# A selective scan in quarters: its B and C rows spread by 32-row selections, the output products written over the states

## The chip, the core and the metric

One core of a Trainium2 chip runs the whole program. PE is TensorE (matmuls), PEld its weight loads, DVE is VectorE, ACT ScalarE, POOL GpSimd, SP SyncE, which here issues the DMAs. The metric is the device time of one execution in microseconds. All matmuls are in fp32, and each shows as two records in the trace, one behind the other.

## The reference

Twelve layers follow one another over x of 4 x 128 tokens and 128 features: four blocks of cross attention, a mixing layer and a feed-forward layer, each `x = x + layer(layernorm(x))`. The change concerns the mixing layer of block 0. With u, the output of a convolution, as 512 tokens of 128 features, it is:

```python
def _selective_scan(u, A_log, D_skip, W_dt, b_dt, W_B, W_C):
    A = -jnp.exp(A_log)
    dt = jax.nn.softplus(u @ W_dt + b_dt)
    Bt = u @ W_B
    Ct = u @ W_C

    def step(h, inp):
        dt_t, B_t, C_t, u_t = inp
        dA = jnp.exp(dt_t[..., None] * A)
        h = dA * h + (dt_t * u_t)[..., None] * B_t[:, None, :]
        y = jnp.einsum('bdn,bn->bd', h, C_t)
        return (h, y)
```

There are 16 states n for each feature, so B and C are 16 rows each over the tokens. The result is y plus u times D_skip, gated, and multiplied by w2.

## The kernel before

The features lie on the 128 partitions, the 4 x 128 tokens side by side in the columns. Everything is written out by hand: one program per engine, and semaphores between them. The stage between U and its result OT runs from about 134 to 198 us.

PE starts with dt's product (L1604). Then `spread(k)` (L1611) makes row n of B or C appear on all 128 partitions: a matmul whose weights are one column of W_B or W_C repeated 128 times, over the 512 columns of U. That takes a full 128-row matmul for each of the 32 rows. The results go round six PSUM banks, so a spread waits until DVE has taken the one six before it (`l0a_bc_taken`). `add_state` (L1617) sums the 16 products over the states, by identity matmuls into bank 1; each waits for its own product.

ACT turns dt (L912) into decays, one exponential over 512 columns per state (L541); POOL then zeroes the first column of each batch in them (L383), so that one scan can run over several states and batches.

DVE works in two halves of eight states. In each it multiplies eight spread B rows by dt times u into DBU (L922), scans all 4096 columns in one instruction, HS from DA and DBU (L926), and multiplies HS by the eight spread C rows, again into DBU (L930). As DBU serves twice, the second half's B products wait for the additions of the first (`l0a_added`). L934 and L937 finish the output once all 16 are added.

The order of PE's work is a list: 14 spreads, then an addition and a spread by turns. In each engine instructions run in the order written, and a wait holds up all that stands behind it. `PE.due(signal, lag=6)` means the count of signals so far less six.

Of the kernel before, what the change touches and what calls it, by code (L numbers as in the profile page):

```python
# [15 lines left out]
ALU = mybir.AluOpType  # L16
# [3 lines left out]
P = 128  # L20
# [69 lines left out]
def build(nc, d, cols, rows):  # L90

    with ExitStack() as ctx:
# [49 lines left out]
        def bank(k, rows_=P):  # L142
            return PSUM[0:rows_, k, :]
# [63 lines left out]
        HS = ARENA[:, 13568:13568 + 4096]  # L207
        SPREAD_BANKS = (4, 5, 6, 7, 0, 2)
# [154 lines left out]
        def _(gpsimd):  # L363
# [15 lines left out]
            for half in range(2):  # L379

                nc.gpsimd.wait_ge(sem("l0a_decay"), PO.due("l0a_decay"))
                cut = DA.rearrange("p (n t) -> p n t", t=P)[:, :, 0:1]
                nc.gpsimd.memset(cut, 0.0).then_inc(sem("l0a_decay_cut"), PO.sends("l0a_decay_cut"))  # L383
# [59 lines left out]
        def _(scalar):  # L443
# [93 lines left out]
            for half in range(2):  # L537
                if half:
                    nc.scalar.wait_ge(sem("l0a_scan"), AC.due("l0a_scan"))
                for n in range(8):  # L540
                    last = act(DA[:, n * 512:(n + 1) * 512], DT, ACT.Exp, scale=ANEG[:, half * 8 + n:half * 8 + n + 1])  # L541
                last.then_inc(sem("l0a_decay"), AC.sends("l0a_decay"))
# [196 lines left out]
        def _(vector):  # L739
# [169 lines left out]
            nc.vector.wait_ge(sem("l0a_preact"), DV.sent("l0a_preact"))  # L909
            nc.vector.wait_ge(sem("l0a_acts"), DV.due("l0a_acts"))  # L910
# [6 lines left out]
            for half in range(2):  # L917
                for n in range(8):
                    nc.vector.wait_ge(sem("l0a_bc"), DV.due("l0a_bc"))
                    if half:  # L920
                        nc.vector.wait_ge(sem("l0a_added"), DV.due("l0a_added"))
                    ve.tensor_tensor(DBU[:, n * 512:(n + 1) * 512], bank(SPREAD_BANKS[(n + half * 16) % 6]), DTU, ALU.mult)\  # L922
                        .then_inc(sem("l0a_bc_taken"), DV.sends("l0a_bc_taken"))
                nc.vector.wait_ge(sem("l0a_bc_taken"), DV.sent("l0a_bc_taken"))
                nc.vector.wait_ge(sem("l0a_decay_cut"), DV.due("l0a_decay_cut"))
                ve.tensor_tensor_scan(HS, DA, DBU, 0.0, ALU.mult, ALU.add).then_inc(sem("l0a_scan"), DV.sends("l0a_scan"))  # L926
                nc.vector.wait_ge(sem("l0a_scan"), DV.sent("l0a_scan"))
                for n in range(8):
                    nc.vector.wait_ge(sem("l0a_bc"), DV.due("l0a_bc"))
                    ve.tensor_tensor(DBU[:, n * 512:(n + 1) * 512], HS[:, n * 512:(n + 1) * 512],  # L930
                                     bank(SPREAD_BANKS[(n + 8 + half * 16) % 6]), ALU.mult)\
                        .then_inc(sem("l0a_bc_taken"), DV.sends("l0a_bc_taken"))
            nc.vector.wait_ge(sem("l0a_added"), DV.due("l0a_added", n=8))
# [494 lines left out]
        def _(tensor):  # L1428
# [175 lines left out]
            mm(bank(3), w("l0a_Wdt"), U, start=True, stop=True).then_inc(sem("l0a_product"), PE.sends("l0a_product"))  # L1604
            def spread(k):

                name, n = ("l0a_WB", "l0a_WC")[k // 8 % 2], k // 16 * 8 + k % 8
                due = PE.due("l0a_bc_taken", lag=6)
                if due is not None:
                    nc.tensor.wait_ge(sem("l0a_bc_taken"), due)  # L1610
                mm(bank(SPREAD_BANKS[k % 6]), w(name)[:, n:n + 1].broadcast_to([P, P]), U, start=True, stop=True)\  # L1611
                    .then_inc(sem("l0a_bc"), PE.sends("l0a_bc"))

            def add_state(half, n):

                nc.tensor.wait_ge(sem("l0a_bc_taken"), 16 * half + 8 + n + 1)
                mm(bank(1), ident, DBU[:, n * 512:(n + 1) * 512], start=half == 0 and n == 0,  # L1617
                    stop=half == 1 and n == 7, skip_group_check=True)\
                    .then_inc(sem("l0a_added"), PE.sends("l0a_added"))


            for half in range(2):
                for k in range(22 * half, 16 * half + 14):
                    spread(k)
                for n in range(8):
                    add_state(half, n)
                    if 16 * half + 14 + n < 32:
                        spread(16 * half + 14 + n)
# [460 lines left out]
def lay_out(i):  # L2089
# [12 lines left out]
    def spread(bias):  # L2102
        out = np.zeros((4, 32, 4), np.float32)
        out[:, :HD, :] = bias.reshape(4, 4, HD).transpose(1, 2, 0)
        return out.reshape(P, 4)
# [12 lines left out]
         ("l0a_Wdt", i["L0_attn_W_dt"]), ("l0a_WB", i["L0_attn_W_B"]), ("l0a_WC", i["L0_attn_W_C"]),  # L2118
# [96 lines left out]
```

## Time and profile before

| what | value |
|---|---|
| runs | 1321.06, 1321.3, 1321.06 us, median 1321.06 |
| profiled execution | 1319.12 us |
| its span | 1317.3 us |
| mean granted clock of TensorE | 0.889 |
| PE busy | 1123.8 us, 85% of the span |
| DVE busy | 619.5 us, 47% |
| ACT busy | 425.8 us, 32% |
| the two scans (L926) | 17.4 us together |
| spreads (L1611), 32 matmuls | 32.7 us |
| additions (L1617), 16 matmuls | 18.5 us |

The span runs from the first to the last instruction in the profile; the execution's time also holds what lies around it. A record's mean length is not the distance to the next one, since neighbouring records overlap on every engine. The granted clock is a share of 2.4 GHz; it has two levels here, 1.00 and 0.50 (1.2 GHz), and a mean in between says how much of a stretch each had.

### The profile page before, as it was taken

How to read it: one execution, taken by the hardware profiler on the slowest of the kernel's cores; microseconds unless marked ns; L12 is line 12 of the kernel's file. 1: busy time of each engine (PE TensorE's matmuls, PEld its weight loads, DVE VectorE, ACT ScalarE, POOL GpSimd, SP SyncE). 2: the span in 40 equal slices, each digit the busy share in tenths (PEclk: the TensorE clock that was granted, in tenths of full speed). 3: DMA queues.
4: the chain of work that ended last, by engine and by line, in shares of the span. 5: the costliest groups of instructions: out<-in, count | busy, mean ns of one | idle time of the engine just before them, and what ended most of it. 6: DMA issues, size and time to landing. Idle time of an engine off the chain costs nothing.

```text
span 1317.3 us, 13027 instructions
## 1 busy us (share of the span) xinstructions
PE 1123.8 (85%) x4766; PEld 642.5 (49%) x4766; DVE 619.5 (47%) x1075; ACT 425.8 (32%) x586; POOL 314.4 (24%) x95
## 2 busy tenths in 40 slices
PE   7996789956899966775867999999999999998558
PEld 4663335734666624443746444544454445444434
DVE  4885754143598842223533443343434344342345
ACT  3663404314465551321125322222322331232011
POOL 0000000000000000000000666556655663665000
PEclk9997789966799985886889999899989998998569
DMA  8100000030000020032000000000000000000100
GB/s 345 76 0 1 0 0 0 1 127 1 0 1 0 1 97 0 0 136 104 1 0 0 17 20 20 15 15 21 20 12 16 20 20 8 21 20 0 70 1 8
DMA packets 21366, 40.15 MB, mean 30 GB/s; under 512 B 2496, under 2 KB 18880, under 8 KB 19648
## 3 DMA queue, kind: packets, MB, share of 16 engines
q1 hardware_dynamic: 21312, 39.41, 8.1%
q8 instruction: 36, 0.59, 0.2%
q14 instruction: 18, 0.15, 0.0%
HBM read 39.14 MB, written 0.26 MB: 30 GB/s over the span
## 4 chain that ended last, share of the span: by engine, by line
PE 78%; DVE 12%; ACT 7%; issue 2%; POOL 1%; DMA 0%; POOLq 0%; DVEq 0%; ACTq 0%
PE PSUM L1933 16%; PE PSUM L1937 16%; PE PSUM L1451 9%; PE PSUM L1659 2%; PE PSUM L1670 2%; PE PSUM L1483 2%; PE PSUM L1962 2%; PE PSUM L1968 1%; PE PSUM L1460 1%; DVE ARENA L926 1%; PE PSUM L2043 1%; PE PSUM L1617 1%; DVE HN L754 1%; PE PSUM L1503 1%; PE PSUM L1518 1%
## 5 line engine op out<-in xcount | busy, mean ns | idle before, releaser
L424 POOL TENSOR_TENSOR ARENA<-ARENA 128x2048 f32<-128x2048 f32 x64 | 288.7, 4511 | 196.6 <-ACT ARENA L684 196.6
L1292 DVE TENSOR_TENSOR ARENA<-PSUM,RK 128x512 f32<-128x512 f32 x256 | 175.7, 691 | 271.8 <-PE PSUM L1933 270.1
L1933 PE MATMUL PSUM<-ARENA,CK 128*128 128x512 f32 x512 | 257.3, 606 | 5.1 <-DVE ARENA L1292 4.3
L1937 PE MATMUL PSUM<-ARENA,CK 128*128 128x512 f32 x512 | 253.0, 597 | 5.8 <-ACT ARENA L706 3.7
L684 ACT ACTIVATE ARENA<-ARENA,CK 128x2048 f32<-128x2048 f32 x64 | 128.1, 2002 | 350.0 <-DVE ARENA L1292 350.0
L1937 PEld LDWEIGHTS PSUM<-ARENA,CK 128*128 128x128 f32 x512 | 97.4, 191 | 132.1 <-issue 112.2
L1933 PEld LDWEIGHTS PSUM<-ARENA,CK 128*128 128x128 f32 x512 | 97.7, 194 | 126.2 <-issue 98.1
L366 POOL TENSOR_TENSOR RSTD<-VE,MHALF 128x4 f32<-128x4 f32 x17 | 17.1, 1009 | 554.5 <-DVE VE L751 554.5
L1451 PE MATMUL PSUM<-WK,CT 128*128 128x512 f32 x256 | 124.1, 607 | 0.0
L454 ACT ACTIVATE SQ<-PSUM 128x512 f32<-128x512 f32 x128 | 76.2, 597 | 67.2 <-PE PSUM L1451 59.4
L773 DVE TENSOR_REDUCE RK<-SQ 128x8 f32<-128x512 f32 x128 | 84.8, 682 | 14.1 <-ACT SQ L454 12.0
L1433 PE MATMUL PSUM<-WA,HN 128*128 128x128 f32 x52 | 14.0, 422 | 79.6 <-DVE HN L754 79.6
L1451 PEld LDWEIGHTS PSUM<-WK,CT 128*128 128x128 f32 x256 | 43.6, 190 | 33.3 <-issue 24.6
L1433 PEld LDWEIGHTS PSUM<-WA,HN 128*128 128x128 f32 x52 | 9.0, 211 | 83.1 <-DVE HN L754 57.9
L446 ACT ACTIVATE HT<-PSUM 128x512 f32<-128x512 f32 x10 | 6.0, 596 | 95.3 <-PE PSUM L1433 95.2
L1611 PE MATMUL PSUM<-ARENA,WB 128*128 128x512 f32 x64 | 32.7, 648 | 0.0
L563 ACT ACTIVATE ARENA<-PSUM,WB 128x512 f32<-128x512 f32 x32 | 22.0, 687 | 29.1 <-PE PSUM L1659 28.3
L1670 PEld LDWEIGHTS PSUM<-CK,ARENA 128*128 128x128 f32 x256 | 29.7, 192 | 3.4 <-issue 3.4
L1659 PE MATMUL PSUM<-HT,CK 128*128 128x512 f32 x64 | 30.9, 610 | 0.0
L1670 PE MATMUL PSUM<-CK,ARENA 128*128 128x128 f32 x256 | 29.7, 275 | 0.0
L987 DVE SCALAR_TENSOR_TENSOR ACC<-PSUM,SM,ACC 128x128 f32<-128x128 f32 x32 | 9.0, 344 | 43.4 <-PE PSUM L1670 43.4
L1617 PE MATMUL PSUM<-ARENA,WA 128*128 128x512 f32 x32 | 18.5, 690 | 11.8 <-DVE ARENA L930 11.8
(388 smaller groups left out, 1412.5 us busy)
## 6 DMA issues: line engine op xcount, KB each, us to landing
CT<-in_ctxT SPq DMA_DIRECT2D x4, 1024.0 KB, 10.9
CK<-in_l0f_experts SPq DMA_DIRECT2D x1, 4096.0 KB, 23.6
CK<-in_ctxk SPq DMA_DIRECT2D x1, 4096.0 KB, 12.1
ARENA<-in_l2f_experts SPq DMA_DIRECT2D x2, 2048.0 KB, 8.2
CK<-in_ctxT SPq DMA_DIRECT2D x64, 64.0 KB, 1.8
CK<-in_ctxr SPq DMA_DIRECT2D x64, 64.0 KB, 1.8
ARENA<-in_l2f_experts SPq DMA_DIRECT2D x1, 3072.0 KB, 14.2
WB<-in_wb SPq DMA_DIRECT2D x1, 2802.5 KB, 11.9
```

Source lines behind the costliest of these rows:

```text
L424: nc.gpsimd.tensor_tensor(LS[b % 2], LS[b % 2], PR[:, k % 2, :], ALU.add)\
L454: act(SQ[:, m % 2, :], bank(5 + 2 * (m % 2)), ACT.Square).then_inc(sem("key_squares"), AC.sends("key_squares"))
L684: act(PR[:, k % 2, :], PR[:, k % 2, :], ACT.Exp, bias=SHIFT).then_inc(sem("l3x_probs"), AC.sends("l3x_probs"))
L773: ve.tensor_reduce(RK[:, m * 8:(m + 1) * 8], SQ[:, m % 2, :].rearrange("p (h e) -> p h e", e=DH), AX.X, ALU.add).then_inc(sem("key_norm"), ...
L1292: ve.tensor_tensor(PR[:, k % 2, c * 512:(c + 1) * 512].rearrange("p (j n) -> p j n", j=4), PSUM[:, c % 2, :].rearrange("p (j n) -> p j n", ...
L1451: mm(bank(5 + 2 * c), CT[:, t * P:(t + 1) * P], WK[:, c * 512:(c + 1) * 512], start=True, stop=True).then_inc(sem("key_rows"), PE.sends("k ...
L1611: mm(bank(SPREAD_BANKS[k % 6]), w(name)[:, n:n + 1].broadcast_to([P, P]), U, start=True, stop=True)\
L1617: mm(bank(1), ident, DBU[:, n * 512:(n + 1) * 512], start=half == 0 and n == 0, stop=half == 1 and n == 7, skip_group_check=True)\
L1659: mm(bank(1 + c % 2), E2[:, e * NW + c * P:e * NW + (c + 1) * P], HT[:, :], start=True, stop=True)\
L1670: last = mm(PSUM[:, 3 + e % 2, b * P:(b + 1) * P], HB[:, e % 2, c, b * P:(b + 1) * P], E2[:, at:at + P], start=c == 0, stop=c == FC - 1)
L1933: mm(bank(c % 2), CTT[:, k, :], qpb[:, b, c * 512:(c + 1) * 512], start=True, stop=True)\
L1937: return mm(bank(4 + c), CKT[:, k, :], PR[:, k % 2, c * 512:(c + 1) * 512], start=first, stop=final, skip_group_check=True)
```

## The change

- The 16 columns each of W_B and W_C lie side by side in one weight, WBC of 32 columns. Four matmuls make B and C of U once for each group of 32 partitions (L1614 of the changed kernel), all into bank 4; DVE copies them to BC (L914).
- A spread is now a matmul over 32 rows of BC, with one column of the identity's 32 x 32 block, repeated 128 times, as weights (L1624). Spread k uses the partitions of row group k mod 4, and four in a row use four groups.
- The scan runs in quarters of four states (2048 columns). DA, DBU and HS have two places each for them. ACT's decays for a quarter wait for the scan two quarters back; POOL's memset comes four times.
- The C products are written over HS (L939), and the additions read HS. DBU waits for no addition any more; the scan of the third and fourth quarter waits for the additions of the quarter two back.
- PE's list is new, as shown below.

```diff
+        BC = ARENA[:, 4736:4736 + 512]
...
-            for half in range(2):
+            for q in range(4):
 
                 nc.gpsimd.wait_ge(sem("l0a_decay"), PO.due("l0a_decay"))
-                cut = DA.rearrange("p (n t) -> p n t", t=P)[:, :, 0:1]
+                cut = DA[:, q % 2 * 2048:(q % 2 + 1) * 2048].rearrange("p (n t) -> p n t", t=P)[:, :, 0:1]
...
-            for half in range(2):
-                if half:
-                    nc.scalar.wait_ge(sem("l0a_scan"), AC.due("l0a_scan"))
-                for n in range(8):
-                    last = act(DA[:, n * 512:(n + 1) * 512], DT, ACT.Exp, scale=ANEG[:, half * 8 + n:half * 8 + n + 1])
+            for q in range(4):
+                due = AC.due("l0a_scan", lag=2)
+                if due is not None:
+                    nc.scalar.wait_ge(sem("l0a_scan"), due)
+                for n in range(4):
+                    at = (q % 2 * 4 + n) * 512
+                    last = act(DA[:, at:at + 512], DT, ACT.Exp, scale=ANEG[:, q * 4 + n:q * 4 + n + 1])
                 last.then_inc(sem("l0a_decay"), AC.sends("l0a_decay"))
...
+            nc.vector.wait_ge(sem("l0a_product"), DV.due("l0a_product"))
+            ve.tensor_copy(BC, bank(4)).then_inc(sem("l0a_bc_rows"), DV.sends("l0a_bc_rows"))
             nc.vector.wait_ge(sem("l0a_acts"), DV.due("l0a_acts"))
...
-            for half in range(2):
-                for n in range(8):
+            for q in range(4):
+                half = slice(q % 2 * 2048, (q % 2 + 1) * 2048)
+                for n in range(4):
+                    at = (q % 2 * 4 + n) * 512
                     nc.vector.wait_ge(sem("l0a_bc"), DV.due("l0a_bc"))
-                    if half:
-                        nc.vector.wait_ge(sem("l0a_added"), DV.due("l0a_added"))
-                    ve.tensor_tensor(DBU[:, n * 512:(n + 1) * 512], bank(SPREAD_BANKS[(n + half * 16) % 6]), DTU, ALU.mult)\
+                    ve.tensor_tensor(DBU[:, at:at + 512], bank(SPREAD_BANKS[(q * 8 + n) % 6]), DTU, ALU.mult)\
                         .then_inc(sem("l0a_bc_taken"), DV.sends("l0a_bc_taken"))
                 nc.vector.wait_ge(sem("l0a_bc_taken"), DV.sent("l0a_bc_taken"))
                 nc.vector.wait_ge(sem("l0a_decay_cut"), DV.due("l0a_decay_cut"))
-                ve.tensor_tensor_scan(HS, DA, DBU, 0.0, ALU.mult, ALU.add).then_inc(sem("l0a_scan"), DV.sends("l0a_scan"))
+                if q >= 2:
+                    nc.vector.wait_ge(sem("l0a_added"), 4 * (q - 1))
+                ve.tensor_tensor_scan(HS[:, half], DA[:, half], DBU[:, half], 0.0, ALU.mult, ALU.add)\
+                    .then_inc(sem("l0a_scan"), DV.sends("l0a_scan"))
                 nc.vector.wait_ge(sem("l0a_scan"), DV.sent("l0a_scan"))
-                for n in range(8):
+                for n in range(4):
+                    at = (q % 2 * 4 + n) * 512
                     nc.vector.wait_ge(sem("l0a_bc"), DV.due("l0a_bc"))
-                    ve.tensor_tensor(DBU[:, n * 512:(n + 1) * 512], HS[:, n * 512:(n + 1) * 512],
-                                     bank(SPREAD_BANKS[(n + 8 + half * 16) % 6]), ALU.mult)\
+                    ve.tensor_tensor(HS[:, at:at + 512], HS[:, at:at + 512], bank(SPREAD_BANKS[(q * 8 + 4 + n) % 6]), ALU.mult)\
                         .then_inc(sem("l0a_bc_taken"), DV.sends("l0a_bc_taken"))
...
+            for j in range(4):
+                last = mm(PSUM[32 * j:32 * j + 32, 4, :], w("l0a_WBC"), U, start=True, stop=True)
+            last.then_inc(sem("l0a_product"), PE.sends("l0a_product"))
+
             def spread(k):
 
-                name, n = ("l0a_WB", "l0a_WC")[k // 8 % 2], k // 16 * 8 + k % 8
+                n = k // 4 % 2 * N + k // 8 * 4 + k % 4
                 due = PE.due("l0a_bc_taken", lag=6)
                 if due is not None:
                     nc.tensor.wait_ge(sem("l0a_bc_taken"), due)
-                mm(bank(SPREAD_BANKS[k % 6]), w(name)[:, n:n + 1].broadcast_to([P, P]), U, start=True, stop=True)\
-                    .then_inc(sem("l0a_bc"), PE.sends("l0a_bc"))
...
+                r = 32 * (k % 4)
+                mm(bank(SPREAD_BANKS[k % 6]), ident[r:r + 32, r + n:r + n + 1].broadcast_to([32, P]), BC[r:r + 32, :],
+                   start=True, stop=True).then_inc(sem("l0a_bc"), PE.sends("l0a_bc"))
+
+            def add_state(q, n):
+
+                nc.tensor.wait_ge(sem("l0a_bc_taken"), 8 * q + 4 + n + 1)
+                at = (q % 2 * 4 + n) * 512
+                mm(bank(1), ident, HS[:, at:at + 512], start=q == 0 and n == 0, stop=q == 3 and n == 3, skip_group_check=True)\
                     .then_inc(sem("l0a_added"), PE.sends("l0a_added"))
 
-
-            for half in range(2):
-                for k in range(22 * half, 16 * half + 14):
-                    spread(k)
-                for n in range(8):
-                    add_state(half, n)
-                    if 16 * half + 14 + n < 32:
-                        spread(16 * half + 14 + n)
+            nc.tensor.wait_ge(sem("l0a_bc_rows"), PE.due("l0a_bc_rows"))
+            for k in range(8):
+                spread(k)
+            for q in range(4):
+                for n in range(4):
+                    if q < 3:
+                        spread(8 * (q + 1) + n)
+                    add_state(q, n)
+                for n in range(4):
+                    if q < 3:
+                        spread(8 * (q + 1) + 4 + n)
```

PE's list in this stage before: the product for dt, spreads (L1611) and additions (L1617), up to w2's product (L1439).

```order
L1604 MATMUL PSUM<-ARENA,WB 128x512
L1611 MATMUL PSUM<-ARENA,WB 128x512 x14
L1617 MATMUL PSUM<-ARENA,WA 128x512
L1611 MATMUL PSUM<-ARENA,WB 128x512
...
L1617 MATMUL PSUM<-ARENA,WA 128x512
L1611 MATMUL PSUM<-ARENA,WB 128x512 x9
L1617 MATMUL PSUM<-ARENA,WA 128x512
L1611 MATMUL PSUM<-ARENA,WB 128x512
...
L1617 MATMUL PSUM<-ARENA,WA 128x512 x6
L1439 MATMUL PSUM<-WB,OT 128x128 x4
```

The same place in the changed kernel: WBC is L1614, a spread L1624, an addition L1631.

```order
L1612 MATMUL PSUM<-ARENA,WB 128x512
L1614 MATMUL PSUM<-ARENA,WB 32x512 x4
L1624 MATMUL PSUM<-ARENA,WA 128x512 x9
L1631 MATMUL PSUM<-ARENA,WA 128x512
L1624 MATMUL PSUM<-ARENA,WA 128x512
...
L1631 MATMUL PSUM<-ARENA,WA 128x512
L1624 MATMUL PSUM<-ARENA,WA 128x512 x5
L1631 MATMUL PSUM<-ARENA,WA 128x512
...
L1624 MATMUL PSUM<-ARENA,WA 128x512 x4
L1631 MATMUL PSUM<-ARENA,WA 128x512 x4
L1447 MATMUL PSUM<-WB,OT 128x128 x4
```

Nine spreads stand ahead of the first addition. Then come three pairs of an addition and a spread, a fourth addition, and five spreads in a row (three times, the last time four), and four additions at the end.

DVE's list before: B products (L922), scan (L926), C products (L930).

```order
L922 TENSOR_TENSOR ARENA<-PSUM,ARENA 128x512 x8
L926 SCALAR_TENSOR_TENSOR ARENA<-ARENA 128x4096
L930 TENSOR_TENSOR ARENA<-ARENA,PSUM 128x512 x8
...
L934 SCALAR_TENSOR_TENSOR ARENA<-ARENA,WB,PSUM 128x512
L937 SCALAR_TENSOR_TENSOR OT<-ARENA 128x512
```

And in the changed kernel, from the copy to BC (L914) on.

```order
L914 COPY ARENA<-PSUM 128x512
L917 SCALAR_TENSOR_TENSOR ARENA<-ARENA 128x512
L920 TENSOR_TENSOR ARENA<-ARENA 128x512
L927 TENSOR_TENSOR ARENA<-PSUM,ARENA 128x512 x4
L933 SCALAR_TENSOR_TENSOR ARENA<-ARENA 128x2048
L939 TENSOR_TENSOR ARENA<-ARENA,PSUM 128x512 x4
...
L942 SCALAR_TENSOR_TENSOR ARENA<-ARENA,WB,PSUM 128x512
L945 SCALAR_TENSOR_TENSOR OT<-ARENA 128x512
```

The triple of products, scan and products stands four times now, with half as much in each part, and the copy is one operation more.

## Rows read from the trace of the kernel before

**Rows 1.** The page: the span, and the chain that ended last, by engine.
```profile
span 1317.3 us, 13027 instructions
...
PE 78%; DVE 12%; ACT 7%; issue 2%; POOL 1%; DMA 0%; POOLq 0%; DVEq 0%; ACTq 0%
```

**Rows 2.** Chain of waits, 120 to 210 us: start us, length us, what, how many.
```profile
142.51 5.02 ACT ARENA L541 x8
147.84 8.70 DVE ARENA L926
...
157.30 2.07 PE PSUM L1617 x2
...
160.67 0.86 PE PSUM L1617 x2
...
171.83 2.59 PE PSUM L1611 x6
174.44 0.70 DVE ARENA L922
175.17 8.70 DVE ARENA L926
...
184.63 2.08 PE PSUM L1617 x2
186.71 1.71 PE PSUM L1611 x2
...
196.59 0.76 DVE ARENA L934
```

**Rows 3.** Table by stage: length, busy us of each engine, granted clock (PEclk), DMA share, GB/s.
```profile
156.53:160.12 3.59, 2.82 (x4) 1.26 (x5) 3.56 (x6) 3.56 (x6) 0.00 (x0) 0.50 0.00 0
183.87:190.84 6.97, 6.21 (x8) 2.59 (x9) 4.36 (x7) 0.00 (x0) 0.00 (x0) 0.51 0.00 0
190.84:196.59 5.75, 5.71 (x14) 2.25 (x12) 0.69 (x1) 0.00 (x0) 0.00 (x0) 1.00 0.00 0
```

**Rows 4.** Groups by form: line, what, count | busy us, mean ns | idle before, releaser.
```profile
L926 DVE TENSOR_TENSOR_SCAN ARENA<-ARENA 128x4096 f32<-128x4096 f32 x2 | 17.4, 8692 | 0.2 <-POOL ARENA L383 0.2
...
L541 ACT ACTIVATE ARENA<-ARENA,SM 128x512 f32<-128x512 f32 x16 | 10.0, 708 | 9.1 <-DVE ARENA L926 9.0
...
L912 DVE SCALAR_TENSOR_TENSOR ARENA<-ARENA 128x512 f32<-128x512 f32 x1 | 0.7, 693 | 3.4 <-ACT ARENA L535 3.4
...
L1159 DVE TENSOR_TENSOR_SCAN ARENA<-ARENA 16x512 f32<-16x512 f32 x1 | 1.2, 1211 | 0.0
```

**Rows 5.** Timeline of the stage, DVE: start us, length us, what, count.
```profile
142.75 4.87 DVE L922 TENSOR_TENSOR ARENA<-PSUM,ARENA 128x512 f32<-128x512 f32 x8
```

**Rows 6.** Timeline, 481.6 to 486.2 us, PE: 32-row and 128-row matmuls by turns.
```profile
482.73 1.13 PE L1771 MATMUL PSUM<-HT,WB 128*128 128x512 f32 x2
...
483.78 1.70 PE L1764 MATMUL PSUM<-ARENA,WB 32*128 32x512 f32 x4
```

**Rows 7.** Timeline, 200 to 320 us, PE: four row groups, then 128 rows.
```profile
297.71 2.09 PE L1483 MATMUL PSUM<-ARENA,QT 8*128 8x512 f32 x8
299.73 3.77 PE L1503 MATMUL PSUM<-WA,ARENA 128*128 128x128 f32 x16
```

**Rows 8.** PE after two idle times: timeline around 495 and 599 us, then table by stage.
```profile
494.90 0.64 PE L1774 MATMUL PSUM<-SM,WA 128*128 128x32 f32 x2 [2.78 <-ACT ARENA L599]
...
599.12 1.12 PE L1812 MATMUL PSUM<-ARENA,WB 128*128 128x512 f32 x2 [3.53 <-DVE ARENA L1159]
...
494.70:495.60 0.90, 0.64 (x2) 0.50 (x2) 0.03 (x1) 0.72 (x3) 0.00 (x0) 0.50 0.00 0
599.10:600.40 1.30, 1.28 (x3) 0.52 (x4) 0.00 (x0) 0.00 (x0) 0.00 (x0) 1.00 0.75 287
600.50:602.00 1.50, 1.50 (x2) 0.00 (x0) 0.00 (x0) 0.00 (x0) 0.00 (x0) 0.50 0.91 265
```

More of the change, by code:

```diff
@@ L925, in _ @@
                 nc.vector.wait_ge(sem("l0a_decay_cut"), DV.due("l0a_decay_cut"))
-                ve.tensor_tensor_scan(HS, DA, DBU, 0.0, ALU.mult, ALU.add).then_inc(sem("l0a_scan"), DV.sends("l0a_scan"))
+                if q >= 2:
+                    nc.vector.wait_ge(sem("l0a_added"), 4 * (q - 1))
+                ve.tensor_tensor_scan(HS[:, half], DA[:, half], DBU[:, half], 0.0, ALU.mult, ALU.add)\
+                    .then_inc(sem("l0a_scan"), DV.sends("l0a_scan"))
                 nc.vector.wait_ge(sem("l0a_scan"), DV.sent("l0a_scan"))
-                for n in range(8):
+                for n in range(4):
+                    at = (q % 2 * 4 + n) * 512
                     nc.vector.wait_ge(sem("l0a_bc"), DV.due("l0a_bc"))
-                    ve.tensor_tensor(DBU[:, n * 512:(n + 1) * 512], HS[:, n * 512:(n + 1) * 512],
-                                     bank(SPREAD_BANKS[(n + 8 + half * 16) % 6]), ALU.mult)\
+                    ve.tensor_tensor(HS[:, at:at + 512], HS[:, at:at + 512], bank(SPREAD_BANKS[(q * 8 + 4 + n) % 6]), ALU.mult)\
                         .then_inc(sem("l0a_bc_taken"), DV.sends("l0a_bc_taken"))
-            nc.vector.wait_ge(sem("l0a_added"), DV.due("l0a_added", n=8))
+            nc.vector.wait_ge(sem("l0a_added"), DV.due("l0a_added", n=16))
             ve.scalar_tensor_tensor(out=Y0, in0=U, scalar=w("l0a_D"), in1=bank(1), op0=ALU.mult, op1=ALU.add)\
@@ L1610, in spread @@
                     nc.tensor.wait_ge(sem("l0a_bc_taken"), due)
-                mm(bank(SPREAD_BANKS[k % 6]), w(name)[:, n:n + 1].broadcast_to([P, P]), U, start=True, stop=True)\
-                    .then_inc(sem("l0a_bc"), PE.sends("l0a_bc"))
[L1614 to L1618, printed above, removed]
-                    .then_inc(sem("l0a_added"), PE.sends("l0a_added"))
-            for half in range(2):
-                for k in range(22 * half, 16 * half + 14):
-                    spread(k)
-                for n in range(8):
-                    add_state(half, n)
-                    if 16 * half + 14 + n < 32:
-                        spread(16 * half + 14 + n)
+                r = 32 * (k % 4)
[5 more added lines that the diff above has]
+                mm(bank(1), ident, HS[:, at:at + 512], start=q == 0 and n == 0, stop=q == 3 and n == 3, skip_group_check=True)\
+                    .then_inc(sem("l0a_added"), PE.sends("l0a_added"))
+            nc.tensor.wait_ge(sem("l0a_bc_rows"), PE.due("l0a_bc_rows"))
[9 more added lines that the diff above has]
+                        spread(8 * (q + 1) + 4 + n)
             nc.tensor.wait_ge(sem("l0a_y"), PE.due("l0a_y"))
@@ L2117, in lay_out @@
          ("l0a_w1", i["L0_attn_w1_w"]), ("l0a_v1", i["L0_attn_v1_w"]), ("l0a_w2", i["L0_attn_w2_w"]),
-         ("l0a_Wdt", i["L0_attn_W_dt"]), ("l0a_WB", i["L0_attn_W_B"]), ("l0a_WC", i["L0_attn_W_C"]),
+         ("l0a_Wdt", i["L0_attn_W_dt"]), ("l0a_WBC", np.concatenate([i["L0_attn_W_B"], i["L0_attn_W_C"]], axis=1)),
          ("l0a_Alog", i["L0_attn_A_log"]), ("l0a_conv", i["L0_attn_conv_w"].reshape(P, 3)),
```

## The prediction

> **What bounds the kernel now.** First the page: PE makes up 78% of the chain that ended last, DVE 12% [rows 1]. That is an average over twelve layers. The change touches one of them, the selective scan, so everything below is read from 134 to 200 us. In the chain of waits for that stretch [rows 2] the reader sees DVE and PE take turns: eight decays on ACT, a scan on DVE (8.70 us), then PE's additions and spreads one behind another until 174.44, the second scan, and PE again until DVE's L934 at 196.59. So neither engine bounds the stage alone. While DVE scans PE runs dry, and after the scan DVE waits for PE. The table by stage [rows 3] gives the third fact: PE ran out of work in both scans and came back at a granted clock of 0.50 (1.2 GHz) both times, for 2.8 us (157.30 to 160.12) and for 6.2 us (184.63 to 190.84), and then had 1.00 (2.4 GHz) again.
>
> The stage falls into four stretches, and I price the change by them: up to the first scan (147.84), two scans of 8.69, one gap between them (156.53 to 175.17, 18.64 us) and the tail from the second scan's end to L934 (183.87 to 196.59, 12.72 us).
>
> **Before the first scan.** New in front are four 32-column products of U (WBC), a copy of them to BC on DVE, and the first spreads, which now wait for that copy. WBC can follow L1604's stream at about 136.7. Its nearest row is four groups at once on half clock, 2.09 us [rows 7], so it is done by 138.8; the copy costs 0.69 like the other DVE operations of this size and ends at 139.5, in DVE's idle time before L912 (3.4 us, waiting for ACT) [rows 4]. Spreads 0 to 3, one in each row group, take another 2.09 and are there at 141.7. DVE asks for the first at 142.75. So these edits are covered with 1 us to spare; if the four did not run side by side, they would take four times 1.71 and the fourth product would be some 2 us late. The scan now needs four decays instead of eight: 142.51 + 3 x 0.61 + 0.71 = 145.05, and from the last decay to the scan passes 0.32, through POOL's memset, as before (147.52 to 147.84) [rows 2, 4]. The four products are ready at 145.2. First scan at 145.4: **-2.5 us**. The second quarter's decays run on under the scan, the third's and fourth's (2.6 us each) wait only for a scan two back and fit under the next one; POOL has four short memsets for two.
>
> **The scans.** Two lengths stand in the trace: 4096 columns 8.692 us and 512 columns (on 16 partitions) 1.211 us [rows 4]. That is 2.087 ns a column and 0.14 fixed, so 4.42 for 2048. Four make 17.67 for 17.38: **+0.3 us**. DVE's 32 products stay 32, at 0.60 each when nothing is late (eight in 4.87) [rows 5]. Writing in place over the states gives them no other size; it lets quarter q+2's scan wait for quarter q's four additions, long done.
>
> **The gaps: three where there was one.** The order on PE decides here. An addition cannot start before its C product, and a spread of the next quarter stands behind each addition: spread 8, add, 9, add, 10, add, 11. Spread 8 runs early, under the scan. The next scan needs the product on spread 11, so each gap holds DVE's first C product and its handoffs (0.03 + 0.68 + 0.05 = 0.75), then six PE steps in a row (add, 9, add, 10, add, 11), then handoff, product, handoff (0.04 + 0.69 + 0.04 = 0.77). Only spreads 12 to 15 stand together, and they run under a scan, where PE had time anyway. So the four row groups shorten nothing in the gap.
> A step between unlike shapes costs more than one between like ones. Like shapes follow at 0.86 on full clock and 1.71 on half [rows 2]. Between 32-row and 128-row matmuls the starts stand 1.05 apart on full clock (482.73 to 483.78) [rows 6] and 2.02 on half (297.71 to 299.73, rows of 8 to 128) [rows 7]. The last step ends 1.13 after its start on full clock, 2.07 on half. A gap is 0.75 + 5 x 1.05 + 1.13 + 0.77 = 7.9 at full clock and 0.75 + 5 x 2.02 + 2.07 + 0.77 = 13.7 at half. Three gaps less the old one: +5.1 or +22.5.
> The Trainium skill, TensorEngine Tiling (Array Packing), section Available Configurations, says that a change of the tiling mode (not of the tile) drains TensorE; the trace agrees in that a switch costs 0.19 more than a like step, though less than a full drain would. A full drain, estimated by that rule with a record's length of 1.13 per step in place of 1.05, would make a gap 8.3 and the sum below 1.2 us larger.
>
> **The tail.** The last quarter has four additions where 22 matmuls' worth of mixed work stood: 0.75 + 4 x 0.86 + 0.3 = 4.5 on full clock, 8.0 on half, for 12.72: -8.2 or -4.7.
>
> **Which clock.** At full clock throughout: -2.5 + 0.3 + 5.1 - 8.2 = **-5.3**. At half clock throughout: -2.5 + 0.3 + 22.5 - 4.7 = **+15.6**. Those are the ends. In each quarter PE has spreads 12 to 15 and 16 after the scan has begun, some 2 us, and then nothing for 4.42 - 2.0 + 0.75 = 3.2 us. The rows nearest to this length are an idle of 2.78 us (PE came back at 0.50) and one of 3.53 us (it came back at 1.00 and had 0.50 some 1.3 us later) [rows 8]. So I take it that the clock falls once in each scan, for about as long as after the two scans of before: the mean of 2.8 and 6.2, 4.5 us. In 4.5 us of half clock 2.2 steps are done that would take 2.3 us at full clock, so 2.2 us are lost, four times: -5.3 + 8.8 = **+3.5**. With 2.8 us each time it is +0.1, with 6.2 us +6.7.
>
> **The sum.** The profiled execution took 1319.12 us, its span of 1317.3 and 1.8 around it, and stands 1.9 under the median of the three runs, 1321.06. With +3.5 it would be 1322.6, and the median 1324.5. What follows the stage is the same code, later by that much; the clock changes there too (it is 0.50 in several stretches after idling [rows 8]), and where its falls land can move by a few microseconds either way. That is in the range.
>
> **Rivals.**
> A, the clock holds: the scans are short enough now that PE keeps 2.4 GHz. For it: idle falls from 5.1 and 6.7 us to 3.2, and after 3.53 us PE did come back at 1.00 [rows 8]. Against: it fell right after, and 2.78 us was enough elsewhere. -5.3, so 1315.8. This is the case on the other side; it decides below some 2.8 us of half clock per gap, where the sum changes sign.
> B, the clock does not come back within a gap: it took 6.2 us of unbroken work after 184.63 [rows 3], and a gap's work is broken at each switch. +15.6, so 1336.7.
> C, switches cost nothing with 32 full rows: steps of 0.86 and 1.71. A gap loses 5 x 0.19 + 0.1 = 1.05 at full clock and some 1.6 at half, about 3.8 in three: 3.5 - 3.8, so 1320.8. Against it stand the rows of L1764 and L1771, which are this very shape.
> D, the change does what its form suggests: PE is always ahead and DVE runs through. Gap 8 x 0.60 + 0.15 = 4.95, three 14.9: -2.5 + 0.3 - 3.7 - 8.2 = -14.1, so 1307. Against it is the order on PE, which lets no spread pass an addition.
>
> **How the numbers follow.** Forecast 0.56, A 0.15, B 0.13, C 0.08, D 0.04, later stages shifting by more than this one 0.04. The predicted time is the forecast's, 1324.5. The range 1315 to 1332 takes in A, C and the forecast with 2.8 to 6.2 us (1321.2 to 1327.8) and a few microseconds of the later stages, and leaves out B and D. Runs differ by 0.02% here, but I call same what lies within 0.2% (2.6 us), about what a measurement can tell. Faster: A 0.15, D 0.04, 0.02 of C, 0.03 of the forecast and the rest: 0.24. Same: the forecast with short falls of the clock 0.20 and most of C: 0.26. Slower: the rest of the forecast 0.35, B 0.13, 0.02 of the rest: 0.50.
>
> **What would show it.** Right: the first scan at 145.4 (covering wrong: later than 146); scans of 4.4; the distance from a scan's end to the next scan 9 to 12 us; PE's starts in the gap 1.05 or 2.02 apart, add and spread by turns; DVE's waits before its B products (L927), not before its C products; the clock at 0.50 at each first addition. Gaps of 8 with the clock at 1.00 mean A, gaps near 14 mean B, starts 0.86 apart mean C, gaps of 5 mean D. The forecast is wrong if PE takes the spreads out of turn, or if L934 comes before 193 or after 206.

## The result and the profile after

The changed kernel takes 1331.79 us (median of 4 runs, 1330.11 to 1333.04), the kernel before 1321.18 beside it (4 runs): ratio 1.0081, 95% interval [1.0066, 1.0096]. It is slower by 10.6 us, where +3.5 was forecast. The profiled execution took 1331.16 us, its span is 1329.4. First the page: the span and the chain that ended last, by engine.

```profile
span 1329.4 us, 13044 instructions
...
PE 78%; DVE 12%; ACT 7%; issue 2%; POOL 1%; DMA 0%; POOLq 0%; DVEq 0%; ACTq 0%
```

These shares are those of [rows 1], and say nothing of the 12.1 us between the spans. The chain of waits of the stage shows where the time went (start us, length us, what, how many).

```profile
137.57 1.56 PE PSUM L1612 x2
...
147.41 4.43 DVE ARENA L933
151.87 0.70 DVE ARENA L939
152.61 2.08 PE PSUM L1631 x2
154.69 2.00 PE PSUM L1624 x2
156.69 2.01 PE PSUM L1631 x2
...
162.70 2.02 PE PSUM L1624 x2
164.74 0.70 DVE ARENA L927
165.47 4.43 DVE ARENA L933
...
182.05 4.43 DVE ARENA L933
...
198.21 4.43 DVE ARENA L933
202.66 0.70 DVE ARENA L939
203.40 5.19 PE PSUM L1631 x8
208.62 0.76 DVE ARENA L942
```

L1612 is the product for dt (L1604 before), L933 a scan, L939 a C product, L1631 an addition, L1624 a spread, L927 a B product, L942 what L934 was. The reader sees six PE steps in a row between a C product and the next scan's last B product, three times, where [rows 2] have one gap. From the dt product on I cut the stage as the prediction did (us):

| | before | after | difference |
|---|---|---|---|
| dt product to first scan | 12.83 | 9.84 | -3.0 |
| scans | 17.39 | 17.72 | +0.3 |
| gaps | 18.64 | 13.63 + 12.16 + 11.73 = 37.52 | +18.9 |
| last scan's end to L934 or L942 | 12.73 | 5.99 | -6.7 |
| stage | 61.59 | 71.04 | +9.45 |
| from there to the end | 1120.73 | 1120.75 | 0.0 |

The other 2.6 us lie ahead of the stage, in unchanged code (the dt product starts at 137.57, before at 135.00). In the profiles of the twelve runs below, whose code is the same up to there, it starts anywhere from 134.96 to 138.29, so nothing ties those 2.6 us to the change.

The clock that each gap had is in the table by stage of the changed kernel (stretch, length, busy us of PE, PEld, DVE, ACT and POOL, granted clock, DMA share, GB/s).

```profile
151.84:165.47 13.63, 12.86 (x13) 3.50 (x14) 5.16 (x9) 2.56 (x4) 0.12 (x1) 0.50 0.00 0
...
168.90:172.30 3.40, 2.44 (x6) 0.59 (x4) 3.37 (x5) 2.38 (x4) 0.00 (x0) 1.00 0.00 0
172.30:182.05 9.75, 9.75 (x11) 2.50 (x10) 2.78 (x5) 0.18 (x1) 0.12 (x1) 0.50 0.01 2
185.90:189.30 3.40, 2.68 (x6) 0.59 (x4) 3.37 (x6) 0.00 (x0) 0.00 (x0) 1.00 0.00 0
189.30:198.21 8.91, 8.91 (x10) 2.50 (x10) 2.28 (x5) 0.00 (x0) 0.00 (x0) 0.50 0.00 0
```

The first gap passes at 0.50 from end to end. The second has 1.00 for one step and part of the next, the third for two steps; then both have 0.50 again, for 9.75 and 8.91 us, although PE is busy in all of that time. Compare [rows 3], where the clock was back after 6.2 us of work behind the second scan. The timeline of PE shows the same (start us, length us, line, operation, count, idle before).

```profile
167.65 2.05 PE L1624 MATMUL PSUM<-ARENA,WA 32*128 32x512 f32 x6
170.67 1.13 PE L1631 MATMUL PSUM<-ARENA,WA 128*128 128x512 f32 x2 [0.96 <-DVE ARENA L939]
171.72 1.55 PE L1624 MATMUL PSUM<-ARENA,WA 32*128 32x512 f32 x2
173.21 2.08 PE L1631 MATMUL PSUM<-ARENA,WA 128*128 128x512 f32 x2
175.21 2.07 PE L1624 MATMUL PSUM<-ARENA,WA 32*128 32x512 f32 x2
```

Starts are 1.05 apart (170.67 to 171.72), then 1.49 where the clock falls, then 2.00 (173.21 to 175.21). Before the first additions of the three gaps and the tail PE idled 4.82, 0.96, 0.72 and 1.93 us, in this order. The rest of the sum stands in the groups by form (count | busy us, mean ns | idle before, releaser).

```profile
L933 DVE TENSOR_TENSOR_SCAN ARENA<-ARENA 128x2048 f32<-128x2048 f32 x4 | 17.7, 4424 | 0.3 <-POOL ARENA L384 0.2
L927 DVE TENSOR_TENSOR ARENA<-PSUM,ARENA 128x512 f32<-128x512 f32 x16 | 10.7, 686 | 22.0 <-PE PSUM L1624 21.9
...
L917 DVE SCALAR_TENSOR_TENSOR ARENA<-ARENA 128x512 f32<-128x512 f32 x1 | 0.7, 692 | 1.5 <-ACT ARENA L536 1.5
L914 DVE COPY ARENA<-PSUM 128x512 f32<-128x512 f32 x1 | 0.7, 691 | 1.1 <-PE PSUM L1614 1.1
```

DVE waits 21.9 us for spreads (L1624) ahead of its B products, and nowhere else in the loop but for 0.2 us ahead of the first scan. The copy (L914) took 0.69 and behind it DVE still idled 1.5 us for ACT, so the copy lies in idle time.

### The profile page after: what moved, and what is told of

Same layout as the page of the kernel before. It is cut to its first block, busy times and chain, and to the rows that moved or that the text cites. A ratio compares the mean times of both kernels' runs of the same rounds, so it can differ in the third digit from the quotient of the medians.

```text
span 1329.4 us, 13044 instructions
## 1 busy us (share of the span) xinstructions
PE 1135.1 (85%) x4774; PEld 638.6 (48%) x4774; DVE 620.4 (47%) x1078; ACT 425.8 (32%) x586; POOL 314.6 (24%) x97
## 4 chain that ended last, share of the span: by engine, by line
PE 78%; DVE 12%; ACT 7%; issue 2%; POOL 1%; DMA 0%; POOLq 0%; DVEq 0%; ACTq 0%
PE PSUM L1949 16%; PE PSUM L1953 16%; PE PSUM L1459 9%; PE PSUM L1675 2%; PE PSUM L1686 2%; PE PSUM L1491 2%; PE PSUM L1631 2%; PE PSUM L1978 1%; PE PSUM L1468 1%; DVE ARENA L933 1%; PE PSUM L1984 1%; PE PSUM L2059 1%; DVE HN L757 1%; PE PSUM L1624 1%; PE PSUM L1511 1%
## 5 line engine op out<-in xcount | busy, mean ns | idle before, releaser
L1631 PE MATMUL PSUM<-ARENA,WA 128*128 128x512 f32 x32 | 28.2, 996 | 8.4 <-DVE ARENA L939 8.4
L1624 PE MATMUL PSUM<-ARENA,WA 32*128 32x512 f32 x64 | 29.9, 944 | 2.5 <-DVE ARENA L927 1.6
## 6 DMA issues: line engine op xcount, KB each, us to landing
ARENA<-in_l2f_experts SPq DMA_DIRECT2D x1, 3072.0 KB, 14.1
```

Source lines behind the costliest of these rows:

```text
L1624: mm(bank(SPREAD_BANKS[k % 6]), ident[r:r + 32, r + n:r + n + 1].broadcast_to([32, P]), BC[r:r + 32, :], start=True, stop=True).then_inc(s ...
L1631: mm(bank(1), ident, HS[:, at:at + 512], start=q == 0 and n == 0, stop=q == 3 and n == 3, skip_group_check=True)\
```

## The experiments

Two things can be at fault: the six serial steps that the order on PE puts into each gap (theory S), and the clock at which PE runs them. "Full spreads" are the 128-row ones of the kernel before, "lead" is the time from the dt product to the first scan, "tail" that from the last scan's end to L942 (L934 before). All kernels are changes of the kernel after or of the kernel before, as said.

**e1_block: the four spreads ahead of the four additions.**

```diff
                 for n in range(4):
                     if q < 3:
                         spread(8 * (q + 1) + n)
+                for n in range(4):
                     add_state(q, n)
```

> The change with PE's list altered alone: the next quarter's four B spreads stand ahead of the four additions instead of between them. If the six serial steps of a gap are the cause (theory S), spreads 10 and 11 follow the first C products at once and a gap falls from about 12 to 13.6 us to DVE's own 8 x 0.60 + 0.15 = 5.0; the stage from L1612 to L942, 71.1 us in the change and 61.6 before, becomes 47 to 51, and the kernel is 10 to 14 us faster than before. If 32-row matmuls and their switches cost by themselves (theory R), or the shorter scans do (theory Q), it stays within 4 us of the change.

Measured: 1307.99 against 1320.09, ratio 0.9897 [0.9877, 0.9918]. Gaps 4.95, 5.53, 4.95, stage 48.56. The stage is 22.5 us shorter than in the kernel after, for a change of order alone. Chain of waits of e1_block around the first gap:

```profile
147.81 4.44 DVE ARENA L933
...
153.01 2.67 PE PSUM L1624 x4
155.68 5.39 PE PSUM L1631 x8
161.08 1.15 PE PSUM L1624 x8
162.23 2.48 DVE ARENA L939 x4
...
167.14 4.44 DVE ARENA L933
```

And from DVE's timeline of e1_block the two places where it waited for C spreads (in brackets the idle time before, and for what):

```profile
162.23 2.48 DVE L939 TENSOR_TENSOR ARENA<-ARENA,PSUM 128x512 f32<-128x512 f32 x4 [0.62 <-PE PSUM L1624]
...
182.13 2.48 DVE L939 TENSOR_TENSOR ARENA<-ARENA,PSUM 128x512 f32<-128x512 f32 x4 [1.20 <-PE PSUM L1624]
```

Between 153 and 162 the chain is on PE, yet the second scan (157.18 to 161.61) passes beside it and is not on the chain. DVE is held only for 0.62 us after that scan, and for 1.20 us after the fourth, where C spreads stand behind additions. Theory S holds, and rival D of the prediction is what this order gives: a gap of 4.95, as D had it.

**e2_full_rows: the order of the change, every spread a 128-row matmul.**

```diff
-                r = 32 * (k % 4)
-                mm(bank(SPREAD_BANKS[k % 6]), ident[r:r + 32, r + n:r + n + 1].broadcast_to([32, P]), BC[r:r + 32, :],
+                mm(bank(SPREAD_BANKS[k % 6]), w("l0a_WBC")[:, n:n + 1].broadcast_to([P, P]), U,
```

> The change with its order, but each spread a 128-row matmul over U as before (the BC product and copy stay and are not used), so PE changes shape nowhere in the gap. Theory R: the gaps shrink by most of what was lost, to below 6 us. Theory S: a gap keeps its six steps, of 0.86 at full clock or 1.71 at half: 6.9 or 12.1 us; as five spreads in a row now fill 4.3 us of each scan, I expect full clock, some 7 us a gap after the first, and a first scan some 2 us later. Stage 54 to 58 us, kernel 3 to 8 us faster than before.

Measured: 1309.02, 0.9905 [0.9883, 0.9927]. Gaps 6.96, 6.95, 6.96, tail 4.51, stage 54.05. Chain of waits of e2_full_rows, first gap:

```profile
151.13 1.12 PE PSUM L1630 x2
152.25 0.86 PE PSUM L1623 x2
...
155.69 0.87 PE PSUM L1623 x2
156.58 0.70 DVE ARENA L927
```

The six steps are there still, at 0.86 each, and the clock has 1.00 from 143.3 to the end of the stage. So in this order the 32-row spreads cost 17.0 us of stage: 3.0 by the switches (7.93, the gap at full clock in e3 below, for 6.95, three times), 13.7 in the gaps and 1.5 in the tail by the clock, less 1.1 that they gain before the first scan. Timeline of PE in e2_full_rows, first addition of the second gap:

```profile
162.51 1.12 PE L1630 MATMUL PSUM<-ARENA,WA 128*128 128x512 f32 x2 [0.81 <-DVE ARENA L939]
```

PE idles 1.68, 0.81, 0.81 and 1.67 us before the three gaps and the tail here, and keeps 1.00; the changed kernel idled 0.96 and 0.72 before its last two gaps and lost it. So the length of the idle time does not tell the two apart. What differs is what PE ran: 128-row matmuls alone, or 32-row ones among them.

**e3_fill: work that keeps the clock, order and shapes of the change.** Five 128-row matmuls ahead of the first addition of quarter 0 and three ahead of that of each later quarter write to a bank that nothing reads (extra work).

```diff
                         spread(8 * (q + 1) + n)
+                    if n == 0:
+                        for _ in range(5 if q == 0 else 3):
+                            mm(bank(3), ident, U, start=True, stop=True)
                     add_state(q, n)
```

> The change with fill: five 128-row matmuls of 512 columns into an unused bank ahead of the first addition, three ahead of the first addition of each later quarter. They are extra work in PE's idle time under the scans. If the half clock after each idle time is what made the forecast too small (theory S with the clock), the granted clock stays 1.00 in the gaps, steps are 1.05 and gaps 7.9, and the stage is some 55 to 58 us, 13 us less than in the change. If the clock has no part in it, the stage gets no shorter, or longer by what the fill sticks out from the scans (up to 5 us).

Measured: 1316.49, 0.9968 [0.9957, 0.9980]. Gaps 10.69, 7.93, 7.93, tail 4.51, the clock 1.00 from 153.7 on. The stage is 59.11, a little over the 55 to 58 expected, since the first gap still had extra work in it that began at 0.50. With 7.93 there too the stage would be 59.11 - 2.76 = 56.35, 5.2 less than before: that is the prediction's -5.3 for a held clock, and its 7.9 a gap. Work for nothing makes the kernel 15 us faster than the change.

**e4_halves_rows: the 32-row spreads alone, in the kernel before.** WBC, its copy and the selection spreads are put in; halves, order and DBU stay.

```diff
-                name, n = ("l0a_WB", "l0a_WC")[k // 8 % 2], k // 16 * 8 + k % 8
+                n = k // 8 % 2 * N + k // 16 * 8 + k % 8
...
-                mm(bank(SPREAD_BANKS[k % 6]), w(name)[:, n:n + 1].broadcast_to([P, P]), U, start=True, stop=True)\
+                r = 32 * (k % 4)
+                mm(bank(SPREAD_BANKS[k % 6]), ident[r:r + 32, r + n:r + n + 1].broadcast_to([32, P]), BC[r:r + 32, :],
+                   start=True, stop=True).then_inc(sem("l0a_bc"), PE.sends("l0a_bc"))
```

> The kernel before with one part of the change: B and C in 32 rows on four row groups, spread by selections; halves, PE's order and the place of the products as before. Theory R and theory S with its switch price: sixteen steps that change shape each time in the gap and six in the tail cost 0.19 more on full clock and 0.31 on half, so 3 to 6 us more, and more where the clock is at half for longer; kernel slower than before by 3 to 9 us. If the four row groups speed up PE on the path, it is faster than before.

Measured: 1339.32, 1.0133 [1.0109, 1.0158]: 19 us slower, where 3 to 9 were expected. The stage is 80.85, and the one gap is 34.85 where it was 18.64. Table by stage of e4_halves_rows: the spreads before the first addition, the gap, and the nine spreads that end it.

```profile
142.46:152.33 9.87, 9.87 (x28) 5.16 (x28) 8.11 (x11) 7.67 (x11) 0.15 (x1) 0.50 0.00 0
159.18:194.03 34.85, 34.08 (x45) 9.68 (x46) 10.40 (x17) 5.01 (x8) 0.15 (x1) 0.50 0.00 0
190.00:196.12 6.12, 6.12 (x19) 2.68 (x18) 3.98 (x4) 0.00 (x0) 0.00 (x0) 0.50 0.00 0
```

PE is busy for 34.08 of 34.85 us and stays at 0.50. Additions and spreads by turns make up 30.1 us of it (159.95 to 190.00, fifteen steps of 2.00). In the kernel before, the same order of like shapes had 1.00 again after 2.8 us [rows 3]. But the first and last lines show 32-row spreads with no addition between them, 9.9 and 6.1 us long, and the clock stays at 0.50 there too. It was 1.00 again only at about 214.6 us, 3.1 us after the last additions began to stand together.

**e5_halves_64 and e6_rows_fill: is it the few rows, and do turns of the two shapes lose a clock that they have?** e5 is e4 with spreads of 64 rows in two groups. e6 is e4 with 128-row matmuls for nothing ahead of the first addition, six in the first half, five in the second (extra work).

```diff
 e5
-                r = 32 * (k % 4)
-                mm(bank(SPREAD_BANKS[k % 6]), ident[r:r + 32, r + n:r + n + 1].broadcast_to([32, P]), BC[r:r + 32, :],
+                r = 64 * (k % 2)
+                mm(bank(SPREAD_BANKS[k % 6]), ident[r:r + 64, r + n:r + n + 1].broadcast_to([64, P]), BC[r:r + 64, :],
 e6
+                for _ in range(6 - half):
+                    mm(bank(3), ident, U, start=True, stop=True)
                 for n in range(8):
                     add_state(half, n)
```

> As e4_halves_rows, in which the clock stayed at 0.50 from before the stage to its end, but each spread over 64 rows (two row groups) instead of 32; the numbers computed are the same. If the pause at each switch of shape keeps the clock down, it stays at 0.50 as in e4: steps 2.0, gap 35 us. If the narrow matmuls do, 64 rows are nearer to 128 and the clock may come back in the gap: some steps of 1.05 and a gap well under 30 us.

> As e4_halves_rows, with six and five 128-row matmuls of 512 columns as extra work ahead of the first addition of each half, under the scans. If the half clock alone makes e4's gap 34.9 us, and alternation at full clock does not lose it, the steps are 1.05 and the gap is 0.75 + 16 x 1.05 + some 2 us = 18.5 to 20, with a stage of 62 to 66 us. If alternation itself makes the clock fall, it shows 0.50 again within the gap and the gap stays above 25 us.

Measured, one run each: e5 1340.12, gap 35.26; e6 1322.1, gap 19.64. Table by stage of e5_halves_64:

```profile
153.90:191.50 37.60, 33.51 (x38) 9.02 (x40) 13.11 (x16) 5.01 (x8) 0.15 (x1) 0.50 0.00 0
191.50:198.30 6.80, 2.78 (x12) 0.95 (x8) 6.52 (x2) 0.00 (x0) 0.00 (x0) 1.00 0.00 0
```

And of e6_rows_fill, its gap, and most of its tail:

```profile
158.88:178.51 19.63, 19.52 (x48) 5.70 (x46) 10.30 (x16) 5.01 (x8) 0.15 (x1) 1.00 0.00 1
187.10:200.70 13.60, 12.72 (x14) 4.12 (x15) 5.16 (x9) 0.00 (x0) 0.00 (x0) 0.50 0.00 0
```

With twice the rows the clock stays down just as long while the shapes alternate (157.99 to 188.04, again 30.1 us). In e5 it came back at 191.5, 3.5 us after the last addition had ended, in a run of 64-row spreads; in e4 it did not come back in such a run of 32-row ones. So e5 doesn't clear the few rows: 64 may be too few as well. Against few rows alone as the cause stands the changed kernel, where the clock came back within 2.3 and 2.7 us of five 32-row spreads in a row (from 166.64 and from 183.23). Which of the two holds the clock down, few rows or the turns, stays open.

In e6 the turns began at 1.00, right behind 128-row work, and held it for 19.6 us, with starts 1.05 apart. That isn't a rule either: in the changed kernel they began at 1.00 twice, behind 0.96 and 0.72 us of idle time, and lost it within two steps. In e6's own second half five matmuls were too few: PE idled 3.84 us behind them, the additions started at 0.50, and the tail took 16.58. The share of pauses doesn't tell the two clocks apart: at 0.50 an unlike step costs 2.00 us against 1.71 for a like one, some 15% of PE's time; at 1.00 it is 1.05 against 0.86, which is no less.

**e7_before_fill: the kernel before, clock held.** The two lines of e6 in the kernel before (extra work).

> The kernel before with that fill alone (six and five matmuls under the two scans). Before lost 2.8 and 6.2 us at half clock after its scans, which is 1.4 and 3.1 us of work. With the clock held the gap falls from 18.6 to about 17.3 us and the tail from 12.7 to 9.6, so the kernel is 4 to 5 us faster than before. If the clock is not what the stage loses there, nothing changes.

Measured: 1314.43 against 1320.4, 0.9951 [0.9934, 0.9968]; gap 17.26 and tail 9.67 for 18.64 and 12.73. Table by stage, gap and tail:

```profile
158.40:176.00 17.60, 16.78 (x39) 7.52 (x40) 10.84 (x18) 5.01 (x8) 0.15 (x1) 1.00 0.00 1
184.00:194.00 10.00, 9.21 (x21) 3.72 (x20) 5.35 (x9) 0.00 (x0) 0.00 (x0) 1.00 0.00 0
```

The stage is 57.15, and the medians are 6.0 apart. So the clock cost the kernel before 4.4 us in this stage, 1.4 behind the first scan and 3.1 behind the second, as expected.

**e8_adds_last: all eight spreads of the next quarter, then the additions.**

```diff
-                for n in range(4):
+                for n in range(8):
                     if q < 3:
                         spread(8 * (q + 1) + n)
+                for n in range(4):
                     add_state(q, n)
-                for n in range(4):
-                    if q < 3:
-                        spread(8 * (q + 1) + 4 + n)
```

> The change with PE's list as: all eight spreads of the next quarter, then the four additions of this one, which then run under the next scan. As e1_block, but no C product should wait for a spread behind additions (e1 waited 0.6 and 1.2 us there). Gaps 4.95 each, tail 4.5 at full clock to 8 at half, stage 47 to 50 us, for 48.6 in e1; kernel 11 to 14 us faster than before.

Measured: 1304.09, 0.9891 [0.9866, 0.9916]; gaps 4.95, 6.01, 4.93, tail 5.97, stage 49.28. The second gap is 1.1 longer than the 4.95 expected of each: no C product waits for a spread any more, but a B product of the third quarter does, 0.98 us, behind the first four additions, which ran mostly at 0.50.

**e9_last_full: the same order, full spreads.** The edit of e2 in e8.

> The order of e8 (all eight spreads of the next quarter, then the four additions), with every spread a 128-row matmul over U as in e2. WBC and its copy are still made and nothing reads the copy. Theory (once the order is right, four row groups pay, because PE's work per quarter has to fit DVE's): DVE needs 4.42 + 4.95 = 9.4 us a quarter, PE 12 like steps of 0.86 = 10.3 at full clock, so PE becomes the bound by about 1 us a quarter, gaps 5.5 to 6.5, but PE never idles and keeps 1.00; lead 11.0 as in e2, tail 4.5. Stage 11.0 + 17.7 + 18 + 4.5 = 51, total 1304 to 1308. Rival (the four row groups are worth nothing in any order): gaps 4.95 and the tail 4.5, stage 48, total under 1304, at least as fast as e8.

Measured: 1307.45 against 1320.75, 0.9916 [0.9888, 0.9944]; gaps 4.95, 4.95, 5.38, tail 5.15, stage 49.16. Chain of waits of e9_last_full:

```profile
151.37 5.42 PE PSUM L1623 x12
156.78 3.43 PE PSUM L1630 x8
160.22 6.87 PE PSUM L1623 x16
167.08 3.43 PE PSUM L1630 x8
170.52 6.87 PE PSUM L1623 x16
177.38 6.88 PE PSUM L1630 x16
...
184.29 0.76 DVE ARENA L942
```

PE is the bound without a break for 32.9 us, 10.3 a quarter, as the theory said, but it had worked ahead by enough that this shows only in the third gap (+0.4) and in the tail (5.15 for 4.5). The stage is as long as e8's. There the row groups gain 1.3 us in the lead (9.71 for 11.04), and half clock takes it back in the second gap and the tail: e8 has 0.50 until about 161.3 and again from 175.6 to 181.8. So neither theory got its number: 49.2 stands between 51 and 48. In this order the row groups are worth nothing in the stage, and in the order of the change they cost 17.0 us. Whether the 3 to 4 us between the totals of e9 and e8 are theirs stays open, since they lie behind the stage (last entry).

**e10_in_place: the output products in place, alone, in the kernel before.**

```diff
-                    if half:
-                        nc.vector.wait_ge(sem("l0a_added"), DV.due("l0a_added"))
...
+                if half:
+                    nc.vector.wait_ge(sem("l0a_added"), DV.due("l0a_added", n=8))
                 ve.tensor_tensor_scan(HS, DA, DBU, 0.0, ALU.mult, ALU.add).then_inc(sem("l0a_scan"), DV.sends("l0a_scan"))
...
-                    ve.tensor_tensor(DBU[:, n * 512:(n + 1) * 512], HS[:, n * 512:(n + 1) * 512],
+                    ve.tensor_tensor(HS[:, n * 512:(n + 1) * 512], HS[:, n * 512:(n + 1) * 512],
...
-                mm(bank(1), ident, DBU[:, n * 512:(n + 1) * 512], start=half == 0 and n == 0,
+                mm(bank(1), ident, HS[:, n * 512:(n + 1) * 512], start=half == 0 and n == 0,
```

> The kernel before with only the output products written in place over the states (HS): the additions read HS, the second half's B products wait for no addition, its scan waits for the eight additions. Theory (PE's order sets the gap, and the wait that moves was never the last one): gap 18.6, tail 12.7, stage 61.6, total within 0.2% of before. Rival (the wait of the B products on the additions held DVE, or the scan's new wait holds it longer): a gap at least 1 us shorter or longer.

Measured: 1320.72 against 1320.75, 1.0017 [0.9994, 1.0039], 10 runs; stage 60.56 (gap 19.08, tail 11.25; the clock comes back later in the gap and earlier in the tail than in the kernel before). Within the 0.4% of the interval, writing in place costs and gives nothing here.

**e11_last_again and e12_block_again: e8 and e1 on one chip.**

> The kernel of e8 once more, in more rounds and on the same chip as e12. Theory: stage 49.3, total 1302 to 1307, and within 2 us of e12, since the two stages differ by less than 1 us. Rival (additions last are worth more than they save in the stage): 3 to 4 us faster than e12, as the two medians stood apart.

> The kernel of e1 once more, beside e11. Theory: stage 48.6, total 1304 to 1308. Rival: as under e11, 1308 with e11 at 1304.

Measured: e11 1303.67, 0.9888 [0.9865, 0.9912], stage 49.98; e12 1306.29, 0.9901 [0.9878, 0.9925], stage 49.07; 6 runs each. The medians stand 2.6 apart, between the two expectations, and the intervals overlap: the best version is one of the two, 14 to 17 us faster than before and, by the medians, 25 to 28 faster than the change. The same code gave stages 0.5 (e1, e12) and 0.7 us (e8, e11) apart, so less than that between two stages says nothing.

The runs of e12 lie in two heaps (1303.43, 1303.99, 1304.77 and 1307.80, 1307.91, 1308.10). The profiled runs of e1 and e12, the same kernel, fell one in each heap, and tell where they part: L942 is followed by 1119.46 us in e1 and 1114.84 in e12. Counted from the start of each span, e12 is 0.7 us behind e1 at L942, 0.7 ahead near 200, 4.7 ahead near 470 and 3.9 ahead from 600 us to the end. From 280 us on the mean granted clock of the two differs (0.91 and 1.00 from 360 to 380 us, e1 first).

## Why the prediction was right or wrong

**Right: sign, range, bound.** Slower had the largest chance, and 1331.79 lies 0.2 us inside the top of 1315 to 1332. That it lies inside is partly luck: the range allowed 6.2 us of half clock per gap, some 12 us lost, and the clock cost 15.2. The bound was read rightly: DVE waits at L927 and not at L939, and its idle time there (21.9 us) is the loss. Of the prediction's own signs, the steps, the scans and the waits came as said. Three others did not. L942 (L934 before) stands at 208.62, beyond 206, and would at 206.05 without the 2.6 us ahead of the stage. The first two gaps, 13.63 and 12.16, are longer than 9 to 12. And the clock was 1.00, not 0.50, at the first addition of the second and third gap.

**Before the first scan.** Forecast -2.5, measured -3.0 (9.84 for 12.83). The four products for WBC ran side by side (1.91 in the chain of e9_last_full, where they stand on the path). The 2.09 taken from [rows 7] is of four groups of rows, while these are four groups of columns, so that the two are alike was not known beforehand. The copy was covered as said: DVE idled 1.5 us behind it. First scan forecast at 145.4, measured at 147.41, of which 2.6 lie ahead of the stage. **Scans**: 4.42 forecast, 4.42 measured.

**The gaps' steps.** 1.05 at full and 2.02 at half clock were forecast from two rows far away, [rows 6] and [rows 7]; 1.05 and 2.00 to 2.01 were measured. A gap at full clock came to 7.93 in e3 (7.9 forecast), one at half to 13.63 (13.7). Rival C (switches cost nothing) is out by these, and by e2's 0.86 for like steps. The Trainium skill, TensorEngine Tiling (Array Packing), section Key Properties (right below the section that the prediction names), has TensorE drained when the tiling mode changes. The runs agree that a switch costs time, 0.19 us at full clock and 0.29 at half, in both directions.

**Which clock: the step that failed.** The prediction took 4.5 us of half clock per gap, the mean of 2.8 and 6.2 after the scans of before, and so 8.8 us for the three gaps and the tail. Measured: 37.52 - 3 x 7.93 = 13.7 in the gaps and 5.99 - 4.51 = 1.5 in the tail, 15.2. Those 6.4 us more, less the 0.5 from the lead, are the 5.9 between +3.5 and +9.45. Two things were wrong in it. First, the idle time: the prediction had PE idle 3.2 us in every scan and the clock fall there once. It left out the fourth addition, which also runs under the scan, and put the spreads behind it at some 2 us; at half clock they took 4.2 us of the second scan together. Measured idle times were 4.82, 0.96, 0.72 and 1.93 us, and in the second and third gap the clock fell after work had begun. Second, and this made the size: the time to recover was carried from 128-row steps to gaps with 32-row spreads among them. Rival B named this ("a gap's work is broken at each switch") and had 0.13. The first gap is B's 13.7 (13.63); in the second and third the clock came back only under the scan, in the run of spreads, and fell again within two steps. In e4 it stays away for the whole gap of 34.85 us. B gives the turns as the reason, and that is not shown: the few rows are left as the other. The warning was in the profile: [rows 3] show 128-row matmuls only, and no row showed a mix recovering. That should have moved the chance from the forecast to B.

**Rival A** (clock holds, sum -5.3) did not happen, but its sum was right (e3: -5.2). **Rival D** (PE ahead, gap 4.95) was excluded rightly by the order and is what e1 has once the order is turned: its stage is 13.0 us shorter than before, for D's 14.1.

**The tail**: -8.2 at full and -4.7 at half forecast, -6.7 measured. **Later stages**: a few microseconds either way were allowed; the profiled run had 0.0.

Of the change's parts by the runs, in us of stage: in place 0 within the noise (e10); the row groups alone +19 (e4), and +17 in the change's own order (e2 against after); quarters with full spreads -7.5 (e2: gaps +2.2, tail -8.2, lead -1.9, scans +0.3). Of these 7.5, up to 4.4 can be the clock that the kernel before lost and e2 kept (e7). The gain of quarters is real, and the 32-row spreads ate it. Either remedy alone, e1's order or e2's full spreads, undoes the loss.

## What to carry to other kernels

Read the order on the waiting engine's supplier step by step: an addition between each two spreads makes every gap a chain of both, and moving four instructions gave 24 us where narrower matmuls gave none. Narrower matmuls that shorten nothing on the critical path can still cost the clock of the work that does count: behind idle times no longer than e2's the change lost it in two gaps, and e2 kept it. Price the clock at the start of each critical stretch, and take the time to recover only from rows of the same mix of shapes.

## What the runs showed of the hardware

- Matmuls of 32 (or 64) rows and 128 rows by turns kept the clock at 0.50 for 30.1 us of unbroken work (e4, e5), and so did 32-row ones alone for 9.9 us (e4), while 128-row ones in the same order had 1.00 after 2.8 and 6.2 us [rows 3]. In the changed kernel 1.00 came back within 2.3 and 2.7 us of 32-row ones. What tells these apart for the chip stays open.
- The same turns begun at 1.00 kept it for 19.6 us behind unbroken 128-row work (e6) and lost it within two steps in the changed kernel.
- PE idle times of 0.81 to 1.68 us left the clock at 1.00 where all matmuls had 128 rows (e2).
- A switch between 32 or 64 rows and 128 rows costs the same in either direction, 0.29 us at half clock for 512 columns (e4, e5); at full clock it is 0.19 for 32 and 128 rows (e6).
- Of one kernel (e12) the runs fall into two heaps some 4 us apart, and the profiles of that kernel (e1, e12) part hundreds of us behind the change, with 0.91 and 1.00 as granted clock from 360 to 380 us. A difference of that size between two kernels needs the stage's own times beside the medians.
